# Experts' lists in a routed feed-forward kernel: rounding up to 128 rows in place of 256

## The chip, the cores and the metric

The kernel runs on one core of one Trainium2 chip. The metric is the device time of one execution in microseconds, the median of several. A profile of one execution goes with it: a span from the first to the last instruction, busy times by engine, and a trace of every instruction.

## What is computed

The reference is one block of a network on 4 sequences of 2048 tokens with 256 features. A time-mixing stage of two layers is followed by a layer norm; then comes a mixture of eight experts, and another layer norm. The expert part is what the change touches:

```python
gate_out = jnp.einsum('bsd,ed->bse', x, Wg)
top_v, top_i = jax.lax.top_k(gate_out, 2)
probs = jax.nn.softmax(top_v, axis=-1)
for e in range(8):
    w_e = jnp.sum(probs * (top_i == e), axis=-1)
    h1 = jnp.einsum('bsd,hd->bsh', x, W1[e])     # 256 -> 512
    h2 = jnp.einsum('bsd,hd->bsh', x, W2[e])     # 256 -> 512
    g = h1 * jax.nn.sigmoid(h1) * h2
    y = jnp.einsum('bsh,dh->bsd', g, W3[e])      # 512 -> 256
    out = out + y * w_e[..., None]
```

Each of the 8192 tokens goes to two experts, so there are 16384 (token, expert) pairs, and how many fall to one expert depends on the data.

## The kernel before, in words

Three phases follow each other: `attention_phase`, `expert_phase`, `norm_phase`. In the first one the router writes every pair (row number, share) into a list per expert in device memory (`slot_list`, 8192 places for each expert). `expert_phase` (line 969) works through these lists in blocks of rows that belong to one expert.

**Blocks.** There are 20 large blocks of 512 rows (`BIG`, line 51), and behind them 31 blocks of 256, 51 in all (`BLOCKS`, line 53). Each expert's list is rounded up to 256 rows. Those numbers are fixed when the program is built; which expert and which part of its list a block takes comes from a small table that VectorE computes (`big_table`, `small_counts`, `fill_table`, lines 117 to 168) and SP reads with `value_load`. Blocks that no expert needs read filler rows and run like the others.

**One block.** GpSimd gathers its rows by an indirect DMA per 128 rows (`gather_rows`, line 83), TensorE transposes them (line 1301), ScalarE rounds them to a high part (`x_hi`) and VectorE subtracts that to get the low part (`x_lo`). Weights are split in the same way, in three parts of 512 KB each (`w_half` on ScalarE, line 1145, and `w_low` on VectorE, line 1198). Each product is then three matmuls: high by high, high by low, low by high. In `hidden` (line 1263) the weights are stationary and the block's rows are the moving side: 48 matmuls of 512 columns for a large block, 48 of 256 columns for a block of 256. So the gated product comes out with the hidden feature on the partitions, which is how the output products (lines 1312 to 1326) want it as their stationary side: 12 matmuls of 256 columns for each 128 rows. A unit is 512 columns of hidden product; a large block has four, a block of 256 has two. The unit's two halves use two of the four banks of `ring`, `silu` and `gated` have two buffers each, and `gate`, `g_hi`, `g_lo` follow on VectorE, ScalarE and VectorE. `weigh` (line 1221) multiplies the output rows by the pairs' shares, and GpSimd adds them to `x_acc` by indirect DMAs, one for 128 rows (line 1126).

**Order of the work.** Every engine runs the same steps, `step(s, ...)`. In step s TensorE does the hidden products of block s, the transposes of block s+1, then the output products of block s-1:

```python
pe.wait_ge(s_xg[1 - j], moved(half + j, tiles))   # line 1295: rows of block s+1
```

GpSimd, in step s, issues the gather for block s+1, and then the adds of block s-2; these wait until the adds of block s-3 have landed (line 1122) and until block s-2 has been weighed (line 1123):

```python
gather_rows(nc, pool, kept, x_src, s_met, half + j, 1 - j, size(1))
if within(s, 2, BLOCKS + 1):
    if within(s, 3, BLOCKS + 1):
        pool.wait_ge(s_add[1 - j], moved(half - 2 + j, size(-3)))
    pool.wait_ge(s_yv, out_banks(s - 1, size(-1)))
```

SP, in step s, issues the list entries and the first two weight parts of block s+2, then the list entries for the adds of block s-1 (after the adds of block s-3 have landed), then the third weight part of block s+2. ScalarE and VectorE keep to a fixed order of their own within the step (lines 1165 and 1229).

The steps at the beginning, at the change of size and at the end are written out; two loops of two steps each cover the rest of the large blocks and the rest of the blocks of 256 (`run`, line 1011).

Of the kernel before, what the change touches and what calls it, by code (L numbers as in the profile page):

```python
# [25 lines left out]
P = 128  # L26
ALU = mybir.AluOpType
# [10 lines left out]
E, H = 8, 512  # L38
# [14 lines left out]
BLOCKS = BIG + (2 * TOKENS - E) // SMALL + E - BIG * (CH // SMALL)  # L53
# [55 lines left out]
def whole_blocks(nc, dve, k, add, bits):  # L109

    table_link(dve, k, nc.vector.tensor_tensor(k.used[:, :], k.base[0:1, :], k.start[:, :], ALU.subtract))
    table_link(dve, k, nc.vector.tensor_scalar(k.used_i[:, :], k.used[:, :], float(add), None, ALU.add))
    table_link(dve, k, nc.vector.tensor_scalar(k.used_i[:, :], k.used_i[:, :], bits, None, ALU.logical_shift_right))
    table_link(dve, k, nc.vector.tensor_copy(k.full[:, :], k.used_i[:, :]))


def fill_table(nc, dve, k, kind, first, n, slots):

    by_expert = [1, n, E]
    past, hop = k.past[:, first:first + n, :], k.hop[:, first:first + n, :]  # L120
    w_row, slot_row = k.rows[:, 0, first:first + n], k.rows[:, 1, first:first + n]
# [9 lines left out]
    table_link(dve, k, nc.vector.scalar_tensor_tensor(slot_row, k.block_no[:, 0:n], float(slots), slot_row,  # L131
                                                      ALU.mult, ALU.add))
    if kind:

        table_link(dve, k, nc.vector.scalar_tensor_tensor(slot_row, k.taken[:, 0:1].to_broadcast([1, n]), float(CH), slot_row,
                                                          ALU.mult, ALU.add))

        table_link(dve, k, nc.vector.tensor_scalar(slot_row, slot_row, float(E * LIST), None, ALU.min))
    nc.vector.tensor_copy(k.table[:, 1, first:first + n], slot_row).then_inc(k.s_table, 1)


def big_table(nc, dve, k):

    dve.wait_ge(k.s_tab, 3)
    whole_blocks(nc, dve, k, 0, CH.bit_length() - 1)
    running_sum(nc, dve, k, k.end[:, 0, :], k.full[:, :])
    table_link(dve, k, nc.vector.memset(k.taken[:, :], 0.0))

    table_link(dve, k, nc.vector.tensor_tensor(k.before[:, :], k.end[:, 0, :], k.full[:, :], ALU.subtract))
    table_link(dve, k, nc.vector.tensor_scalar(k.before[:, :], k.before[:, :], -1.0, float(BIG), ALU.mult, ALU.add))  # L150
    table_link(dve, k, nc.vector.tensor_scalar(k.before[:, :], k.before[:, :], 0.0, None, ALU.max))
    table_link(dve, k, nc.vector.tensor_tensor(k.taken[:, 0:E], k.before[:, :], k.full[:, :], ALU.min))
    running_sum(nc, dve, k, k.end[:, 0, :], k.taken[:, 0:E])
    table_link(dve, k, nc.vector.tensor_scalar(k.skip[:, 0, :], k.taken[:, 0:E], -float(CH), float(LIST), ALU.mult, ALU.add))
    fill_table(nc, dve, k, 0, 0, BIG, CH)


def small_counts(nc, dve, k):

    whole_blocks(nc, dve, k, SMALL - 1, SMALL.bit_length() - 1)  # L160
    table_link(dve, k, nc.vector.scalar_tensor_tensor(k.used[:, :], k.taken[:, 0:E], -float(CH // SMALL), k.full[:, :],
                                                      ALU.mult, ALU.add))
    running_sum(nc, dve, k, k.end[:, 1, :], k.used[:, :])

    table_link(dve, k, nc.vector.scalar_tensor_tensor(k.skip[:, 1, :], k.taken[:, 1:E + 1], float(CH), k.skip[:, 0, :],
                                                      ALU.mult, ALU.add))
    table_link(dve, k, nc.vector.scalar_tensor_tensor(k.skip[:, 1, :], k.used[:, :], -float(SMALL), k.skip[:, 1, :],
                                                      ALU.mult, ALU.add))
# [800 lines left out]
def expert_phase(nc, w_ffn, x_src, x_acc, slot_list, kept):  # L969
    ident, table, pair_in, xg = kept.ident, kept.table, kept.pair_in, kept.xg  # L970
    s_w, s_pair, s_xg = kept.s_w, kept.s_pair, kept.s_xg
    with ExitStack() as ctx:
# [30 lines left out]
        s_h, s_silu, s_g, s_gh, s_gl = sem("h_product"), sem("silu_ready"), sem("gated_ready"), sem("gh_ready"), sem("gl_ready")  # L1003
        s_y, s_yv = sem("y_product"), sem("y_weighted")
# [4 lines left out]
        block = ctx.enter_context(nc.Block())  # L1009

        def run(eng, step):
# [4 lines left out]
            def peeled(first, end):  # L1016
                for s in range(first, end):
                    step(s, s // 2, s % 2, lambda d: Q if s + d < BIG else Q // 2)

            def loop(first, end, size):  # L1020
                with eng.Fori(first // 2, end // 2) as it:
                    step(it * 2, it, 0, size)
                    step(it * 2 + 1, it, 1, size)

            last = (BLOCKS - 2) // 2 * 2
            peeled(-1, 4)
            loop(4, BIG - 2, lambda d: Q)
            peeled(BIG - 2, BIG + 4)
            loop(BIG + 4, last, lambda d: Q // 2)
            peeled(last, BLOCKS + 2)  # L1030

        def banks_before(b, tiles, full):

            if isinstance(b, int):
                return full * min(b, BIG) + full // 2 * max(b - BIG, 0)
            return b * full if tiles == Q else b * (full // 2) + full // 2 * BIG

        def hidden_units(b, tiles):

            return banks_before(b, tiles, HC)  # L1040

        def row_units(b, tiles):

            return banks_before(b, tiles, DC)

        def out_banks(b, tiles):

            return banks_before(b, tiles, 2)

# [458 lines left out]
```

## Time and profile before

| | |
|---|---|
| Median of three runs | 1239.77 us (1239.7 to 1246.08) |
| Profiled execution | 1232.79 us, span 1230.9 us |
| TensorE busy | 1112.7 us (90%), weight loads 987.3 us (80%) |
| VectorE, ScalarE, GpSimd busy | 916.7 us (74%), 622.2 us (51%), 696.8 us (57%) |
| Expert phase | from about 530 to 1180 us of the span |
| Indirect DMAs in it | 142 gathers, 142 adds |

A busy TensorE is not TensorE at its peak: its instructions overlap, so rates are read from the distance between the starts of two matmuls. The granted clock of TensorE is 1.00 at 2.4 GHz and 0.50 at 1.2 GHz. An instruction of GpSimd that starts an indirect DMA is shown as long as the issue takes; when the data has landed shows at whoever waits for it.

### The profile page before, as it was taken

What the parts mean: (1) busy time and instruction counts of PE and PEld (TensorE: products, weight loads), DVE (VectorE), ACT (ScalarE), POOL (GpSimd) and SP (SyncE); (2) the same over time, 40 slices, a digit from 0 to 9 for tenths busy, and PEclk for the clock granted to TensorE, in tenths of its full rate; (3) what the DMA queues carried; (4) which work ended last, traced back from release to release, by engine and by line L of the source; (5) the groups of instructions that cost most, each with busy time, mean ns of one, the idle gap of its engine ahead of it and who ended that gap; (6) DMA issues with size and microseconds to landing.
All of it is one profiled execution on the core that took longest, in us unless ns stands there. A gap on an engine that the chain in (4) does not pass through costs nothing. (4 is left out here: it accounts for less than half of the span.)

```text
span 1230.9 us, 22912 instructions
## 1 busy us (share of the span) xinstructions
PE 1112.7 (90%) x6916; PEld 987.3 (80%) x6916; DVE 916.7 (74%) x2031; ACT 622.2 (51%) x1027; POOL 696.8 (57%) x572
## 2 busy tenths in 40 slices
PE   6999999999999998669999999999999999999900
PEld 6778877777777786558888888888989999999900
DVE  5788888888888886656766666666668887888737
ACT  4344454444444443254544454445456665666528
POOL 1012544444444543676666766677577776777634
PEclk9999999999999999779999999999999999999965
DMA  4011222111121111467665765576579988889559
GB/s 154 18 52 52 52 52 53 52 55 53 60 54 52 51 35 36 121 148 192 144 153 138 166 156 136 142 169 157 126 186 232 242 223 226 244 227 244 117 175 388
DMA packets 80660, 164.17 MB, mean 133 GB/s; under 512 B 27424, under 2 KB 45600, under 8 KB 80352
## 3 DMA queue, kind: packets, MB, share of 16 engines
q1 hardware_dynamic: 49248, 126.16, 33.9%
q0 software_dynamic: 31360, 37.38, 16.2%
q8 instruction: 25, 0.41, 0.2%
q14 instruction: 27, 0.22, 0.1%
HBM read 118.01 MB, written 45.49 MB: 133 GB/s over the span
## 5 line engine op out<-in xcount | busy, mean ns | idle before, releaser
L1126 POOL DMA_INDIRECT x_acc<-fy_sb,pair_out x142 | 285.6, 2012 | 149.4 <-DVE fy_sb L1227 68.9
L1282 PE MATMUL fring<-fxh,fw_hi 128*128 128x256 f32 (+1 forms) x816 | 265.9, 326 | 3.6 <-DVE fxl L1218 2.0
L1284 PE MATMUL fring<-fxh,fw_lo 128*128 128x256 f32 (+1 forms) x816 | 266.2, 326 | 0.0
L1283 PE MATMUL fring<-fxl,fw_hi 128*128 128x256 f32 (+1 forms) x816 | 265.6, 325 | 0.0
L1145 ACT ACTIVATE fw_hi<-w_raw 128x1024 fp32r<-128x1024 f32 x153 | 161.2, 1054 | 148.4 <-PE fy L1325 140.1
L1198 DVE TENSOR_TENSOR fw_lo<-w_raw,fw_hi 128x1024 fp32r<-128x1024 f32 x153 | 186.5, 1219 | 17.4 <-ACT fw_hi L1145 17.3
L509 POOL TENSOR_TENSOR rs<-ve,neg_half 128x4 f32<-128x4 f32 x48 | 55.6, 1158 | 253.8 <-DVE nm L596 253.8
L88 POOL DMA_INDIRECT xg<-x_src,pair_in x142 | 159.9, 1126 | 43.3 <-issue 42.1
L78 POOL DMA_INDIRECT slot_list<-pairs,slot_u x128 | 145.5, 1137 | 50.9 <-issue 35.2
L1282 PEld LDWEIGHTS fring<-fxh,fw_hi 128*128 128x128 f32 x816 | 154.0, 189 | 17.0 <-ACT fxh L1163 4.2
L1283 PEld LDWEIGHTS fring<-fxl,fw_hi 128*128 128x128 f32 x816 | 154.2, 189 | 13.3
L1284 PEld LDWEIGHTS fring<-fxh,fw_lo 128*128 128x128 f32 x816 | 154.2, 189 | 13.2
L1323 PE MATMUL fy<-fw_hi,gh 128*128 128x256 f32 x568 | 164.0, 289 | 0.0
L833 PE MATMUL ring<-xh,w_hi 128*128 128x512 f32 x384 | 160.6, 418 | 2.2 <-issue 2.0
L1325 PE MATMUL fy<-fw_hi,gl 128*128 128x256 f32 x568 | 159.8, 281 | 0.0
L1324 PE MATMUL fy<-fw_lo,gh 128*128 128x256 f32 x568 | 159.8, 281 | 0.0
L834 PE MATMUL ring<-xl,w_hi 128*128 128x512 f32 x384 | 153.5, 400 | 0.0
L835 PE MATMUL ring<-xh,w_lo 128*128 128x512 f32 x384 | 153.2, 399 | 0.0
L1207 DVE TENSOR_TENSOR gated<-fring,silu 128x512 f32<-128x512 f32 x142 | 98.2, 691 | 70.0 <-PE fring L1284 70.0
L1158 ACT ACTIVATE gh<-gated 128x512 fp32r<-128x512 f32 x142 | 89.6, 631 | 82.8 <-DVE gated L1207 82.8
L1212 DVE TENSOR_TENSOR gl<-gated,gh 128x512 fp32r<-128x512 f32 x142 | 97.4, 686 | 15.4 <-ACT gh L1158 15.4
L1324 PEld LDWEIGHTS fy<-fw_lo,gh 128*128 128x128 f32 x568 | 108.7, 191 | 0.0
(135 smaller groups left out, 1966.2 us busy)
## 6 DMA issues: line engine op xcount, KB each, us to landing
w_raw<-w_ffn SPq DMA_DIRECT2D x153, 512.0 KB, 4.7
x_in<-h SPq DMA_DIRECT2D x16, 512.0 KB, 3.4
x_src<-x SPq DMA_DIRECT2D x16, 512.0 KB, 4.5
x_acc<-x SPq DMA_DIRECT2D x16, 512.0 KB, 5.7
acc<-x_acc SPq DMA_DIRECT2D x16, 512.0 KB, 7.5
out<-o SPq DMA_DIRECT2D x16, 512.0 KB, 6.5
xg<-x_src,pair_in POOLq DMA_INDIRECT x142
x_acc<-fy_sb,pair_out POOLq DMA_INDIRECT x142
```

What stands on the lines that cost most here:

```text
L88: nc.gpsimd.indirect_dma_start(kept.xg[j][:, q, :], None, x_src, bass.IndirectOffsetOnAxis(kept.pair_in[j][:, q, 0:1].bitcast(U32), 0)).th ...
L833: nc.tensor.matmul(out, hi, xh[l][:, dc, :], start=dc == 0, stop=False)
L834: nc.tensor.matmul(out, hi, xl[l][:, dc, :], start=False, stop=False)
L1126: nc.gpsimd.indirect_dma_start(x_acc, bass.IndirectOffsetOnAxis(pair_out[j][:, q, 0:1].bitcast(U32), 0), y[j][:, q, :], None, compute_op=A ...
L1145: nc.scalar.activation(w_hi[:, j, low:high], w_raw[:, j, low:high], ACT.Copy).then_inc(s_whi[i], 1)
L1198: nc.vector.tensor_tensor(w_lo[:, j, low:high], w_raw[:, j, low:high], w_hi[:, j, low:high].bitcast(F32), ALU.subtract).then_inc(s_wlo[i], 1)
L1282: nc.tensor.matmul(out, hi, rows_hi, start=dc == 0, stop=False)
L1283: nc.tensor.matmul(out, hi, rows_lo, start=False, stop=False)
L1284: last = nc.tensor.matmul(out, lo, rows_hi, start=False, stop=dc == DC - 1)
L1323: nc.tensor.matmul(out, a, hi, start=hc == 0, stop=False)
L1324: nc.tensor.matmul(out, a, lo, start=False, stop=False)
L1325: last = nc.tensor.matmul(out, c, hi, start=False, stop=hc == HC - 1)
```

## The change

The lists are rounded up to 128 rows. At most 135 blocks of 128 rows can then be needed; they are laid out as 20 blocks of 512, 24 of 256 and 8 of 128 (136 tiles of 128 rows in place of 142). The order is: six large blocks; eight times one large block and one single of 128; six large blocks; the 24 of 256. That makes 52 blocks, with singles at 7, 9, ... 21.

In a single the sides of the hidden product are swapped: its rows are stationary and the weights move, 512 columns at a time, so that a half takes 6 matmuls and fills one bank. The gated product then has rows on the partitions, and TensorE transposes it in four pieces into ring bank 2 at the end of the step, behind the output products of the block before; ScalarE and VectorE take the high and the low part from there. The output products of a single are 12 matmuls.

The counts that the waits need are now computed from the list of sizes (class `Spot`); the table has three kinds of blocks, filled in steps 3 and 4 by VectorE. The order of operations on GpSimd and SP within a step stays as it was. The diff, cut to its core:

```diff
+TILES_MAX = (2 * TOKENS + E * (P - 1)) // P
+SINGLES = E
+PAIRS = (TILES_MAX - BIG * Q - SINGLES + 1) // 2
+SIZES = [Q] * 6 + [Q, 1] * SINGLES + [Q] * (BIG - SINGLES - 6) + [2] * PAIRS
+BLOCKS = len(SIZES)
+UNITS = {Q: HC, 2: HC // 2, 1: 1}
+ROW_BANKS = {Q: DC, 2: 1, 1: 1}
+OUT_BANKS = {Q: 2, 2: 1, 1: 1}
...
         def _(pool):
...
                     if within(s, 1, BLOCKS):
-                        pool.wait_ge(s_pt, row_units(s, size(0)))
-                    gather_rows(nc, pool, kept, x_src, s_met, half + j, 1 - j, size(1))
+                        pool.wait_ge(s_pt, spot.before(ROW_BANKS, 0))
+                    gather_rows(nc, pool, kept, x_src, s_met, half + j, 1 - j, spot.size(1))
                 if within(s, 2, BLOCKS + 1):
...
-                        pool.wait_ge(s_add[1 - j], moved(half - 2 + j, size(-3)))
-                    pool.wait_ge(s_yv, out_banks(s - 1, size(-1)))
+                        pool.wait_ge(s_add[1 - j], spot.moved(-3))
+                    pool.wait_ge(s_yv, spot.before(OUT_BANKS, -1))
...
+            def g_hi(b, j, u, spot):
+                v = spot.before(UNITS, 0) + u
+                if spot.size(0) == 1:
+                    act.wait_ge(s_gt, spot.before({Q: 0, 2: 0, 1: 1}, 1))
+                    src = ring[2][:, :]
...
+            def g_lo(j, u, spot):
+                dve.wait_ge(s_gh, spot.before(UNITS, 0) + u + 1)
+                src = ring[2][:, :] if spot.size(0) == 1 else gated[:, u % 2, :]
...
                 if within(s, 1, BLOCKS):
-                    weigh(s - 1, half - 1 + j, 1 - j, size(-1))
+                    weigh(half - 1 + j, 1 - j, spot)
+                if units == 1:
+                    g_lo(j, 0, spot)
                 if at(s, 2):
-                    small_counts(nc, dve, kept)
+                    rest_counts(nc, dve, kept)
                 if at(s, 3):
-                    fill_table(nc, dve, kept, 1, BIG, BLOCKS - BIG, SMALL)
+                    rest_starts(nc, dve, kept)
+                    fill_table(nc, dve, kept, 1)
+                if at(s, 4):
+                    fill_table(nc, dve, kept, 2)
...
+                        behind = u == 0 and spot.size(-1) == 1
                         if i == 0:
-                            pe.wait_ge(s_silu, v - 1)
+                            pe.wait_ge(s_silu, v if behind else v - 1)
+                            if u == 1 and spot.size(-1) == 1:
+                                pe.wait_ge(s_gl, v - 1)
...
+                    if tiles == 1:
+                        out = ring[i][:, :]
+                        for dc in range(DC):
+                            col = PART[i][0] + dc * H
+                            hi, lo = w_hi[:, j, col:col + H], w_lo[:, j, col:col + H]
+                            rows_hi, rows_lo = xh[:, dc * P:(dc + 1) * P], xl[:, dc * P:(dc + 1) * P]
+                            nc.tensor.matmul(out, rows_hi, hi, start=dc == 0, stop=False)
+                            nc.tensor.matmul(out, rows_hi, lo, start=False, stop=False)
+                            last = nc.tensor.matmul(out, rows_lo, hi, start=False, stop=dc == DC - 1)
+                        last.then_inc(s_h, 1)
+                        continue
...
+                if within(s, 0, BLOCKS - 1) and spot.size(0) == 1:
+                    pe.wait_ge(s_g, spot.before(UNITS, 1))
+                    for hc in range(HC):
+                        last = nc.tensor.transpose(ring[2][:, hc * P:(hc + 1) * P], gated[:, 0, hc * P:(hc + 1) * P], ident[:, :])
+                    last.then_inc(s_gt, 1)
```

## Rows read from the trace of the kernel before

**Rows 1.** Busy time by stretch: PE, PEld, DVE, ACT, POOL, PEclk, DMA share, GB/s

```profile
545.00:895.00 350.00, 347.86 (x2091) 307.41 (x2090) 230.70 (x317) 171.49 (x259) 240.81 (x159) 1.00 0.64 151
930.00:1170.00 240.00, 238.25 (x2029) 237.59 (x2028) 194.80 (x239) 151.63 (x210) 172.38 (x104) 1.00 0.84 217
```

**Rows 2.** Who waited for whom, TensorE, 545 to 1180: total, times, longest

```profile
PE ftp L1301 <- DMA xg<-x_src,pair_in: 5.2, 4, 3.1
PE fring L1282 <- ACT fxh L1163: 1.6, 1, 1.6
```

**Rows 3.** Timeline of TensorE, one large step: start, duration, instruction

```profile
673.25 0.39 PE L1282 MATMUL fring<-fxh,fw_hi 128*128 128x512 f32 x1
...
684.24 1.03 PE L1301 MATMUL ftp<-ident,xg 128*128 128x128 f32 x8
685.03 0.36 PE L1323 MATMUL fy<-fw_hi,gh 128*128 128x256 f32 x1
...
690.76 0.40 PE L1282 MATMUL fring<-fxh,fw_hi 128*128 128x512 f32 x1
```

**Rows 4.** Timeline of VectorE: weighing instructions four blocks of 256 apart

```profile
926.94 0.69 DVE L1227 TENSOR_TENSOR fy_sb<-fy,pair_out 128x512 f32<-128x512 f32 x1
...
962.63 0.68 DVE L1227 TENSOR_TENSOR fy_sb<-fy,pair_out 128x512 f32<-128x512 f32 x1
```

**Rows 5.** Timeline of VectorE: first table instruction of step 3, next weight split

```profile
603.97 0.39 DVE L123 TENSOR_TENSOR past<-block_no,end 1x248 f32<-1x248 f32 x1
...
606.87 1.23 DVE L1198 TENSOR_TENSOR fw_lo<-w_raw,fw_hi 128x1024 fp32r<-128x1024 f32 x1
```

**Rows 6.** Timeline of VectorE and GpSimd behind that large step

```profile
690.96 0.69 DVE L1227 TENSOR_TENSOR fy_sb<-fy,pair_out 128x512 f32<-128x512 f32 x1 [2.13 <-PE fy L1325]
...
692.50 2.27 POOL L1126 DMA_INDIRECT x_acc<-fy_sb,pair_out  x1 [3.04 <-issue]
...
706.25 0.95 POOL L88 DMA_INDIRECT xg<-x_src,pair_in  x1 [0.30 <-issue]
```

**Rows 7.** Timeline of GpSimd and TensorE, from large blocks to blocks of 256

```profile
885.02 2.35 POOL L1126 DMA_INDIRECT x_acc<-fy_sb,pair_out  x1 [5.50 <-DVE fy_sb L1227]
...
898.73 2.65 POOL L1126 DMA_INDIRECT x_acc<-fy_sb,pair_out  x1 [2.66 <-DMA x_acc<-fy_sb,pair_out]
...
909.99 0.98 POOL L88 DMA_INDIRECT xg<-x_src,pair_in  x1 [0.30 <-issue]
...
909.49 0.28 PE L1284 MATMUL fring<-fxh,fw_lo 128*128 128x256 f32 x1
912.84 0.66 PE L1301 MATMUL ftp<-ident,xg 128*128 128x128 f32 x4 [3.07 <-DMA xg<-x_src,pair_in]
```

**Rows 8.** Timeline of GpSimd and TensorE, a later wait among blocks of 256

```profile
1017.85 1.76 POOL L88 DMA_INDIRECT xg<-x_src,pair_in  x1 [0.30 <-issue]
...
1022.98 0.66 PE L1301 MATMUL ftp<-ident,xg 128*128 128x128 f32 x4 [0.93 <-DMA xg<-x_src,pair_in]
```

**Rows 9.** Timeline of SP's DMA queue during the wait in rows 7

```profile
911.52 0.33 SPq L1078 DMA_DIRECT2D w_raw<-w_ffn  x1
```

**Rows 10.** Busy time by stretch (columns of rows 1) and TensorE's timeline, behind that wait

```profile
914.00:917.00 3.00, 3.00 (x16) 3.00 (x15) 2.42 (x3) 0.65 (x2) 2.56 (x2) 0.50 1.07 195
917.00:918.00 1.00, 1.00 (x8) 1.00 (x8) 0.05 (x1) 0.00 (x0) 0.83 (x1) 0.78 0.97 366
...
914.66 0.42 PE L1323 MATMUL fy<-fw_hi,gh 128*128 128x256 f32 x1
...
916.58 0.42 PE L1323 MATMUL fy<-fw_hi,gh 128*128 128x256 f32 x1
```

**Rows 11.** TensorE's timeline and busy time by stretch, the second large block

```profile
548.00 1.10 PE L1301 MATMUL ftp<-ident,xg 128*128 128x128 f32 x8 [0.52 <-DMA xg<-x_src,pair_in]
550.71 0.47 PE L1282 MATMUL fring<-fxh,fw_hi 128*128 128x512 f32 x1 [1.62 <-ACT fxh L1163]
...
547.00:551.00 4.00, 1.86 (x12) 1.20 (x11) 2.37 (x4) 2.31 (x4) 3.08 (x4) 1.00 0.23 10
```

More of the change, by code:

```diff
@@ L1025, in run @@
+            mixed_end = 6 + 2 * SINGLES
+            pairs_from = BLOCKS - PAIRS
             last = (BLOCKS - 2) // 2 * 2
[L1026 to L1029, printed above, removed]
+            peeled(-1, 10)
+            loop(10, mixed_end - 2)
+            peeled(mixed_end - 2, pairs_from + 4)
+            loop(pairs_from + 4, last)
             peeled(last, BLOCKS + 2)
[L1032 to L1036, printed above, removed]
@@ L1069, in pairs @@
+            def pairs(spot, d, dst, j, done):
+                tiles = spot.size(d)
+                row = first_row(1, spot, d, SLOTS - CH)
                 return sp.dma_start(dst[j][:, 0:tiles, :], slot_list[bass.ds(row, tiles * P), :]
@@ L1160, in x_hi @@
[L1160 to L1166 removed]
+            def g_hi(b, j, u, spot):
+                v = spot.before(UNITS, 0) + u
+                if spot.size(0) == 1:
+                    act.wait_ge(s_gt, spot.before({Q: 0, 2: 0, 1: 1}, 1))
+                    src = ring[2][:, :]
+                else:
+                    act.wait_ge(s_g, v + 1)
+                    src = gated[:, u % 2, :]
+                if within(b, 2, BLOCKS):
+                    act.wait_ge(s_y, spot.before(OUT_BANKS, -1))
+                nc.scalar.activation(gh[:, j, u * CH:(u + 1) * CH], src, ACT.Copy).then_inc(s_gh, 1)
@@ new lines, in x_hi, with step @@
+            def x_hi(spot, d):
+                for i in range(ROW_BANKS[spot.size(d)]):
+                    n = width(spot.size(d))
+                    act.wait_ge(s_pt, spot.before(ROW_BANKS, d) + i + 1)
+                    nc.scalar.activation(xh[:, i * n:(i + 1) * n], tp[i][:, 0:n], ACT.Copy).then_inc(s_xh, 1)
+            def step(s, half, j, spot):
+                here, nxt = within(s, 0, BLOCKS - 1), within(s, -1, BLOCKS - 2)
+                units = UNITS[spot.size(0)] if here else 0
@@ L1229, in step @@
-            def step(s, half, j, size):
-                here, nxt, units = within(s, 0, BLOCKS - 1), within(s, -1, BLOCKS - 2), unit_count(size(0))
+                for k in range(OUT_BANKS[tiles]):
+                    bank, n = (j if tiles == 2 else k), min(tiles, 2)
+                    dve.wait_ge(s_y, spot.before(OUT_BANKS, -1) + k + 1)
+                    share = pair_out[j][:, 2 * k:2 * k + n, 1:2].bitcast(F32).to_broadcast([P, n, D])
+                    nc.vector.tensor_tensor(y[j][:, 2 * k:2 * k + n, :], yp[bank][:, 0:n, :], share, ALU.mult).then_inc(s_yv, 1)
@@ L1231, in step @@
+            def step(s, half, j, spot):
+                here, nxt = within(s, 0, BLOCKS - 1), within(s, -1, BLOCKS - 2)
+                units = UNITS[spot.size(0)] if here else 0
                 if here:
                     w_low(2, s, j)
-                    gate(s, 0, size(0))
+                    gate(s, 0, spot)
                 if nxt:
                     w_low(0, s + 1, 1 - j)
-                if here:
-                    g_lo(s, j, 0, size(0))
-                    gate(s, 1, size(0))
@@ L1239, in step @@
[L1239 to L1251 removed]
+                if units > 1:
+                    g_lo(j, 0, spot)
+                    gate(s, 1, spot)
```

307 lines of the change are left out of this document (163 added, 144 removed).

## The prediction

> **What bounds the kernel now.** I read the table of busy time by stretch first. The change touches only the expert stage, and there TensorE is busy in 347.86 of 350 us while blocks of 512 rows run and in 238.25 of 240 us while blocks of 256 run, at the full clock in both [rows 1]; DMA queues and VectorE have room (shares of 0.64 and 0.84, 230.70 us and 194.80 us). So a block costs what its matmuls cost, unless TensorE has to wait. The waits list says on what: 5.2 us in all, in four waits, the longest 3.1 us, always for gathered rows (xg) [rows 2]. I read the change from those two ends: how many matmuls go, and which gathers come too late.
>
> One step of a large block is then read from TensorE's timeline [rows 3]: the hidden products start at 673.25 and end where the transposes start, 684.24 (10.99 us, 48 matmuls of 512 columns, 0.229 us each); the eight transposes take 0.79 us; the output products of the block before run from 685.03 to 690.76 (5.73 us, 48 matmuls of 256 columns, 0.119 us each). The step is 17.51 us. In the stretch of 256-row blocks the weighing instruction comes at 926.94 and, four blocks later, at 962.63 [rows 4]: 8.92 us for a block.
>
> **What is removed and added on TensorE.** 31 blocks of 256 become 24, so 7 x 8.92 = 62.4 us go. Eight blocks of 128 come. Each has 12 matmuls of 512 columns (12 x 0.229 = 2.75), 12 of 256 (12 x 0.119 = 1.43), two transposes of its rows (a quarter of 0.79, 0.20) and four of the gated product (half of 0.79, 0.40): 4.78 us, eight of them 38.2 us. On TensorE alone the change is worth 38.2 - 62.4 = -24.2 us.
>
> **What hides the rest of a small block.** A single block still loads, splits and subtracts whole expert weights. VectorE works 230.70/350 x 17.51 = 11.5 us in a large step and 194.80/240 x 8.92 = 7.2 us in one of 256; a single has no more than the latter, so a pair of steps (large, single) has at most 18.7 us of VectorE work in 22.3 us of TensorE work. For the DMA queues the same reckoning gives 11.2 + 7.5 = 18.7 us. Neither ends last. The gated product of a single goes to ring bank 2 only after the output products of the large block before it (5.73 us), long after its gate; its high and low parts (one ScalarE and one VectorE instruction) are due before the next block's second unit, 12 matmuls of 0.229 us later; I cost that wait at nothing, and at under 1 us if VectorE is late. The table for the rest of the lists was a run of small VectorE instructions from 603.97 to the next weight split at 606.87 [rows 5], with no TensorE wait in that stretch [rows 2]; the new third step has 20 such instructions in place of 10, most of them on 8 elements. I cost them at nothing too, and at 1 us if they push a gate past the unit that needs its bank.
>
> **What is late: the gather behind the adds.** GpSimd issues, in order, the gather for block s+1 and then the adds of block s-2 (lines 1113 to 1128). A gather therefore stands behind the adds of the step before. In a large step the second weighing starts at 690.96, the four adds follow at 692.50 and the four gathers behind them end at 706.25 + 0.95 = 707.20 [rows 6]: 1.54 + 14.70 us. There the rows are needed only after the next large hidden product, so nothing waits. At the one place where steps become short, the first blocks of 256, it does wait: GpSimd's last gather begins at 909.99 and is issued by 910.97, TensorE has been done since 909.77 (909.49 + 0.28) and starts its transposes at 912.84, 1.87 us after the issue's end [rows 7]. The new order makes such a place of each single. After a large block A and a single B, the large block C is wanted at the end of B's hidden product, and its gather stands behind the four adds of the large block before A.
>
> I work the loop from second weighing to second weighing. The gather path: 1.54 + 14.70 (adds and gathers) + 1.87 (landing) + 0.79 (transposes of C) + 5.73 (output products of A) + 0.20 (to its second weighing, 690.96 against 690.76) = 24.83 us. TensorE's own path for the same two steps is 17.51 + 4.78 = 22.29 us. So TensorE waits 2.5 us in each such pair of steps. The first single (block 7) is free: block 5 before its neighbour is large, so the step of block 6 lasts 10.99 + 0.20 + 5.73 = 16.9 us, and the gather for block 8 has landed 18.1 us after the weighing at that step's start, 1.3 us before TensorE asks for it. The second (block 9) pays more: the adds of block 6 must wait until those of block 5 have landed, and between two such starts 13.71 us passed (885.02 to 898.73) [rows 7]. From the second weighing of block 5: 1.54 + 13.71 + 14.70 + 1.87 = 31.8 us until block 10 has its rows; TensorE is ready after -0.20 + 2.75 + 0.79 + 5.73 + 0.40 (single 7's step) + 10.99 + 0.20 + 1.43 + 2.75 (large 8, single 9) = 24.8 us: a wait of 7.0 us. Sum of waits: 7.0 + 6 x 2.5 = 22.0 us. The landing is the term with bounds. While weights crowd the queues in the 256-row stretch, a gather begun at 1017.85 and issued by 1019.61 let TensorE go at 1022.98, 3.37 us [rows 8]; I take 1.87, since in the new steps as in [rows 7] just one weight part is issued beside the gather (at 911.52 there) [rows 9]. The bounds are 7 x 1.5 = +10.5 us above and, for adds and gathers that are issued 1 us sooner, 7 us below.
>
> The Trainium skill (DMA: Bandwidth & Descriptors, Anatomy of one DMA) puts a GpSimd-issued DMA at about 2.0 us plus its bytes over 436 GB/s, an estimate of 2.3 us for one gather of 128 KB. [Rows 7] show 2.85 us from the beginning of the last gather to the transposes, so the trace is slower than the page; by the page every wait would be 0.55 us shorter and the sum below 3.9 us lower, and the measurement decides.
>
> **What a wait does to the clock.** After the wait of 3.07 us the granted clock fell to 0.50 from 914 to 917 and was 0.78 in the next microsecond, so 3.4 us at 1.2 in place of 2.4 GHz [rows 10]; matmuls of 256 columns then started 0.213 us apart (914.66 to 916.58, nine of them), so 16 of them cost 16 x (0.213 - 0.119) = 1.5 us more. Two idle times of 0.52 and 1.62 us close to each other left the clock at 1.00 from 547 to 551 [rows 11]. The 7.0 us wait will pay 1.5 us. The six of 2.5 us lie about midway between 2.14 and 3.07 us, so I let half of them pay: 4 x 1.5 = 6.0 us in all, with 1.5 and 10.5 us as ends.
>
> **Sum.** -62.4 + 38.2 + 22.0 + 6.0 = +3.8 us. The profiled execution took 1232.79 us around a span of 1230.9; the median of the runs is 1239.77, 7 us above it. I lay the difference on the median: 1243.6 us. A difference of 0.5% (6.2 us) is about what a measurement of this kernel can tell from no change.
>
> **Rivals.** (1) The clock falls at every wait and the gathers land as late as in the 256-row stretch. All seven pay: 7 x 1.5 = 10.5 in place of 6.0 gives +8.3, 1248 us; with landings later by 1.5 us it is up to +18.8, 1258.6 us. For it: 2.5 us is not far from 3.07. Against it: 2.5 us is shorter than the one wait that a fall followed, and the queues are less full here. It decides from the point where five or more of the six waits pay. The Trainium skill (TensorE: Matmul & The Clock Gate, HAM oscillation) describes a kernel whose clock falls at each wait for a transfer, tile after tile; by that rule all seven pay. Chance 0.37.
> (2) The waits don't form, or only the first does, because the adds are issued faster once the steps alternate, or a gather lands while the last transposes of the single run. Without any wait the time is 1239.8 - 24.2 = 1215.6 us; with waits of half the size and the first one's clock, -24.2 + 11.0 + 1.5 = -11.7, 1228 us. For it: TensorE's work does go. Against it: the wait at 909.77 happened in this very order of instructions, with only two gathers behind the four adds. Chance 0.20.
> (3) The forecast, within about 6 us of before: 0.43. That the change does less than it says is no case: the number of blocks of each size is fixed when the program is built, and empty ones run like full ones.
>
> The forecast's own range is 1236 to 1246 us. Eight times in ten the time should lie between 1226 us (half the waits) and 1257 us (all clocks, most landings late). Faster by over 0.5%: 0.20; within: 0.43; slower: 0.37.
>
> **What would show it.** In the changed profile TensorE should be at full clock and busy through the six leading large blocks and the first single, then idle about 7 us for xg in the step of block 9 and about 2.5 us in each of six more single steps, with clock of 0.5 after some; waits of TensorE for xg should sum to some 25 us instead of 5.2. Between the starts of two runs of four adds some 24.8 to 26.5 us should pass. The stretch of 24 blocks should keep 8.9 us a block. I am wrong if TensorE waits for something else (split weights, the low part of the gated product), if the gathers are in time, or if a single block's own matmuls take more than 4.8 us.

## The result, and the profile after

The changed kernel takes 1229.22 us (median of 20 runs, 1220.58 to 1235.75) beside 1241.59 us of the kernel before on the same chip (20 runs): a ratio of 0.9897, 95% interval 0.9879 to 0.9915. That is 12.4 us less, where 3.8 us more was forecast; 1229.22 us lies outside the forecast's own range (1236 to 1246 us), though inside the wide one (1226 to 1257 us). The profiled execution took 1233.89 us, span 1232.0 us; it holds one stop of 13 us, which the last of the experiments takes up, and without it would have been faster than the median.

Busy time by stretch, the columns as in [rows 1]:

```profile
545.00:895.00 350.00, 327.71 (x1902) 285.02 (x1901) 237.56 (x347) 177.44 (x263) 208.86 (x151) 0.97 0.66 169
930.00:1170.00 240.00, 236.19 (x1964) 232.78 (x1963) 185.83 (x228) 145.25 (x201) 167.22 (x102) 0.99 0.80 203
```

TensorE is no longer busy all through the 350 us of the first stretch; 22 us of it are idle. The waits list of the expert stage says where (in all, times, longest):

```profile
PE fring L1366 <- ACT fxh L1223: 13.1, 1, 13.1
PE ftp L1385 <- DMA xg<-x_src,pair_in: 12.1, 9, 6.8
```

13.1 us are the one stop. Gathered rows cost 12.1 us in nine waits, one of them 6.8 us, against the 25 us that the prediction wanted to see. TensorE's timeline has the long wait just where it was forecast, in the step of the second single, and shows what became of the others:

```profile
702.19 1.97 PE L1385 MATMUL ftp<-ident,xg 128*128 128x128 f32 x8 [6.82 <-DMA xg<-x_src,pair_in]
...
734.33 0.60 PE L1417 MATMUL fring<-ident,gated 128*128 128x128 f32 x4
...
750.90 1.09 PE L1385 MATMUL ftp<-ident,xg 128*128 128x128 f32 x8 [0.28 <-DMA xg<-x_src,pair_in]
751.75 0.36 PE L1409 MATMUL fy<-fw_hi,gh 128*128 128x256 f32 x1
...
757.49 0.60 PE L1417 MATMUL fring<-ident,gated 128*128 128x128 f32 x4
```

The first wait is 6.82 us (forecast 7.0), and the eight transposes behind it take 1.97 us at the lower clock instead of 1.09. But the ones after it are 0.27, 0.28, 0.29, 0.20, 0.34 and 0.32 us (forecast 2.5 each). From one transposition of the gated product to the next, 734.33 to 757.49, a pair of steps takes 23.16 us. GpSimd's timeline of that pair, with VectorE's under it, shows why:

```profile
736.26 1.58 POOL L1176 DMA_INDIRECT x_acc<-fy_sb,pair_out  x1 [6.72 <-issue]
738.15 1.56 POOL L1176 DMA_INDIRECT x_acc<-fy_sb,pair_out  x1 [0.30 <-issue]
740.02 1.72 POOL L1176 DMA_INDIRECT x_acc<-fy_sb,pair_out  x1 [0.30 <-issue]
742.04 1.84 POOL L1176 DMA_INDIRECT x_acc<-fy_sb,pair_out  x1 [0.30 <-issue]
744.19 1.01 POOL L98 DMA_INDIRECT xg<-x_src,pair_in  x1 [0.30 <-issue]
...
748.03 0.99 POOL L98 DMA_INDIRECT xg<-x_src,pair_in  x1 [0.30 <-issue]
```

```profile
734.53 0.69 DVE L1291 TENSOR_TENSOR fy_sb<-fy,pair_out 128x512 f32<-128x512 f32 x1 [1.23 <-PE fy L1411]
735.60 0.69 DVE L1273 TENSOR_TENSOR gl<-fring,gh 128x512 fp32r<-128x512 f32 x1 [0.38 <-ACT gh L1217]
736.55 1.23 DVE L1258 TENSOR_TENSOR fw_lo<-w_raw,fw_hi 128x1024 fp32r<-128x1024 f32 x1 [0.26 <-ACT fw_hi L1196]
```

Four adds and four gathers take 12.76 us here (736.26 to 748.03 + 0.99), and 12.76 to 12.97 us in all six of the steps with a short wait, not the 14.70 us of [rows 6]. The add that took 2.27 us there takes 1.58 us here.

### The profile page after: what moved, and what is told of

It reads as the page before. It is cut to its first block and busy times, and to the rows that moved or that the text cites. A ratio compares the mean times of both kernels' runs of the same rounds, so it can differ in the third digit from the quotient of the medians.

```text
span 1232.0 us, 21935 instructions
## 1 busy us (share of the span) xinstructions
PE 1094.7 (89%) x6624; PEld 959.7 (78%) x6624; DVE 913.2 (74%) x2050; ACT 618.3 (50%) x1019; POOL 657.9 (53%) x560
## 5 line engine op out<-in xcount | busy, mean ns | idle before, releaser
L1176 POOL DMA_INDIRECT x_acc<-fy_sb,pair_out x136 | 258.8, 1903 | 187.0 <-DVE fy_sb L1291 103.0
L1366 PE MATMUL fring<-fxh,fw_hi 128*128 128x256 f32 (+1 forms) x704 | 234.9, 334 | 15.3 <-ACT fxh L1223 13.1
L1368 PE MATMUL fring<-fxh,fw_lo 128*128 128x256 f32 (+1 forms) x704 | 233.9, 332 | 0.0
L1367 PE MATMUL fring<-fxl,fw_hi 128*128 128x256 f32 (+1 forms) x704 | 233.3, 331 | 0.0
L98 POOL DMA_INDIRECT xg<-x_src,pair_in x136 | 148.7, 1093 | 44.4 <-issue 39.6
L1366 PEld LDWEIGHTS fring<-fxh,fw_hi 128*128 128x128 f32 x704 | 133.2, 189 | 29.0 <-ACT fxh L1223 13.3
L1368 PEld LDWEIGHTS fring<-fxh,fw_lo 128*128 128x128 f32 x704 | 133.1, 189 | 13.5
L1367 PEld LDWEIGHTS fring<-fxl,fw_hi 128*128 128x128 f32 x704 | 133.0, 189 | 13.1
L1217 ACT ACTIVATE gh<-gated 128x512 fp32r<-128x512 f32 x128 | 80.8, 631 | 81.2 <-DVE gated L1267 76.9
L1409 PEld LDWEIGHTS fy<-fw_hi,gh 128*128 128x128 f32 x544 | 104.1, 191 | 0.0
```

The source lines that it names most:

```text
L1176: nc.gpsimd.indirect_dma_start(x_acc, bass.IndirectOffsetOnAxis(pair_out[j][:, q, 0:1].bitcast(U32), 0), y[j][:, q, :], None, compute_op=A ...
L1366: nc.tensor.matmul(out, hi, rows_hi, start=dc == 0, stop=False)
L1367: nc.tensor.matmul(out, hi, rows_lo, start=False, stop=False)
L1368: last = nc.tensor.matmul(out, lo, rows_hi, start=False, stop=dc == DC - 1)
L1409: nc.tensor.matmul(out, a, hi, start=hc == 0, stop=False)
```

## The experiments

**Does the issue of an add depend on VectorE, or on the queues?** These are VectorE's splits of the weights (fw_lo) and GpSimd's adds behind [rows 6], in the kernel before:

```profile
692.06 1.23 DVE L1198 TENSOR_TENSOR fw_lo<-w_raw,fw_hi 128x1024 fp32r<-128x1024 f32 x1 [0.40 <-ACT fw_hi L1145]
694.55 1.22 DVE L1198 TENSOR_TENSOR fw_lo<-w_raw,fw_hi 128x1024 fp32r<-128x1024 f32 x1
697.33 1.22 DVE L1198 TENSOR_TENSOR fw_lo<-w_raw,fw_hi 128x1024 fp32r<-128x1024 f32 x1
```

```profile
695.08 2.15 POOL L1126 DMA_INDIRECT x_acc<-fy_sb,pair_out  x1 [0.30 <-issue]
697.53 2.45 POOL L1126 DMA_INDIRECT x_acc<-fy_sb,pair_out  x1 [0.30 <-issue]
700.29 1.55 POOL L1126 DMA_INDIRECT x_acc<-fy_sb,pair_out  x1 [0.30 <-issue]
```

The add at 692.50 starts while the split (692.06 + 1.23) has 0.79 us to go and takes 2.27 us; with 0.69 us left an add takes 2.15, with 1.02 left 2.45, and with no such instruction running 1.55. In the changed kernel the low part of the single's product (gl at 735.60) comes ahead of the split on VectorE, and its high part (gh) comes ahead of the rounding of the weights on ScalarE (fw_hi), for which the split then waits 0.26 us. So the split starts 0.29 us after the add. Theory T1 makes what is left of VectorE's instruction the cause; T2 blames the weights on the DMA queues. T1's edit leaves most of the split out:

```diff
 def w_low(i, b, j):
     low, high = PART[i]
+    if not (isinstance(b, int) and b < 2):
+        high = low + 64
     dve.wait_ge(s_whi[i], b + 1)
     ...
```

> The kernel before, with VectorE's subtraction for the low parts of the weights cut to 64 columns from the third block on (most of the low weights are left out, so the products lack their low terms). Theory T1 (an add's issue on GpSimd takes about 1.55 us plus what is left of a VectorE instruction with two SBUF operands that is running when it starts): adds of 1.55 to 1.6 us all through the large blocks instead of 2.27, 2.15, 2.45, 1.55, and from the start of the first add to the end of the last gather about 12.5 us instead of 14.7. Theory T2 (crowded DMA queues lengthen the issue): unchanged, 14.5 to 14.7 us. The time itself should move little by either, by at most some 3 us, since TensorE's instructions stay.

T2's edit leaves most of the weights' transfers out:

```diff
 def weights(b, j, i, w_row):
     low, high = PART[i]
     if within(b, 2, BLOCKS):
...
+        high = low + 64
```

> The kernel before, with each weight transfer cut to 64 columns per part from the third block on (most of the weights are not loaded, so the products are of other weights). T2 (crowded DMA queues lengthen the adds' issue): adds and gathers of a large step about 12.5 us instead of 14.7. T1 (VectorE's two-operand instructions do): 14.5 to 14.7 us as before. The landing of the gathers in the 256-row stretch, up to 3.37 us from issue's end to TensorE's start, should fall towards 1.9 us by either, if crowding is its cause.

GpSimd's timeline of a large step, with the short split (the first fence, with one row of VectorE's under it) and with the short transfers (the last):

```profile
700.05 1.62 POOL L1126 DMA_INDIRECT x_acc<-fy_sb,pair_out  x1 [4.29 <-issue]
701.97 1.59 POOL L1126 DMA_INDIRECT x_acc<-fy_sb,pair_out  x1 [0.30 <-issue]
...
705.73 2.05 POOL L1126 DMA_INDIRECT x_acc<-fy_sb,pair_out  x1 [0.30 <-issue]
...
711.94 0.94 POOL L88 DMA_INDIRECT xg<-x_src,pair_in  x1 [0.30 <-issue]
```

```profile
705.66 0.69 DVE L1214 TENSOR_TENSOR gl<-gated,gh 128x512 fp32r<-128x512 f32 x1 [0.57 <-ACT gh L1158]
```

```profile
694.34 2.27 POOL L1127 DMA_INDIRECT x_acc<-fy_sb,pair_out  x1 [3.04 <-issue]
696.92 2.15 POOL L1127 DMA_INDIRECT x_acc<-fy_sb,pair_out  x1 [0.30 <-issue]
699.37 2.45 POOL L1127 DMA_INDIRECT x_acc<-fy_sb,pair_out  x1 [0.30 <-issue]
702.13 1.55 POOL L1127 DMA_INDIRECT x_acc<-fy_sb,pair_out  x1 [0.30 <-issue]
...
708.09 0.95 POOL L88 DMA_INDIRECT xg<-x_src,pair_in  x1 [0.31 <-issue]
```

With hardly any weights in the queues (busy for 0.40 of 720 to 860 us, not 0.64) the four adds keep their durations to the hundredth of a microsecond, and the whole is 14.70 us again: T2 falls. The landing may depend on the queues: after one wait of 1.89 us at the first blocks of 256 none follows, where three profiles of the kernel before with whole transfers have two or three more, of 0.55 to 1.92 us. With one profile this is likely, and not shown. With the short split the first three adds are 1.56 to 1.62 us and the whole 12.83 us (13.22 and 13.03 in the steps beside it): T1 stands. The fourth add, 2.05 us, started while another VectorE instruction with both operands in SBUF (gl from gated and gh) had 0.62 us left. So the rule is 1.55 us plus what is left of it, less about 0.1 us; I had expected 12.5 us because I had counted the split alone. Over all fourteen profiles the rule has its counterpart too: 218 adds of the expert phase start beside a VectorE instruction with an operand in PSUM, and they take 1.55 to 1.63 us. The times, 1236.42 and 1231.65 us beside 1234.46, say nothing more, as expected.

The Trainium skill (SBUF — State Buffer, SBUF: two separate sides) says that VectorE and GpSimd share a port pair as an exclusive lock, and that a VectorE instruction with two SBUF inputs takes it only against a GpSimd instruction that reads SBUF. That a DMA issued by GpSimd can't get its descriptors written is told there of VectorE's 2-port modes, and not of such an instruction. These rows agree with a lock held to the instruction's end (2.05 us beside 0.62 us left), and show it for the issue of an indirect DMA, which the Trainium skill doesn't name there; no run here tells what in the issue needs the lock.

**The same in the changed kernel.** The edit is that of the short split. GpSimd's timeline has two rows of VectorE's under it.

> The changed kernel with VectorE's subtraction for the low weights cut to 64 columns from the third block on (most of the low weights are left out). Theory T1 (the add's issue is lengthened by VectorE's two-operand instructions): from the first add to the end of the last gather in an alternating pair of steps about 12.3 us instead of 12.76, so the six waits of 0.3 us vanish; the first wait falls from 6.8 to about 3 to 5 us, since the large steps before it lose some 2 us of adds each. If waits and issue times stay as they are, T1 has no part in them in this order of steps.

```profile
733.55 1.58 POOL L1176 DMA_INDIRECT x_acc<-fy_sb,pair_out  x1 [7.03 <-issue]
735.43 1.56 POOL L1176 DMA_INDIRECT x_acc<-fy_sb,pair_out  x1 [0.30 <-issue]
737.30 1.55 POOL L1176 DMA_INDIRECT x_acc<-fy_sb,pair_out  x1 [0.30 <-issue]
739.15 1.55 POOL L1176 DMA_INDIRECT x_acc<-fy_sb,pair_out  x1 [0.30 <-issue]
741.01 1.02 POOL L98 DMA_INDIRECT xg<-x_src,pair_in  x1 [0.30 <-issue]
742.33 1.27 POOL L98 DMA_INDIRECT xg<-x_src,pair_in  x1 [0.30 <-issue]
...
745.16 1.15 POOL L98 DMA_INDIRECT xg<-x_src,pair_in  x1 [0.30 <-issue]
```

```profile
735.17 0.69 DVE L1269 TENSOR_TENSOR gated<-fring,silu 128x512 f32<-128x512 f32 x1 [1.11 <-PE fring L1370]
...
742.05 0.69 DVE L1275 TENSOR_TENSOR gl<-gated,gh 128x512 fp32r<-128x512 f32 x1 [0.70 <-issue]
```

All four adds are at the floor, 6.24 us instead of 6.70, as T1 has it; the second starts 0.26 us into a gated (735.17 + 0.69), which reads one operand from PSUM, and isn't lengthened. But the sum is 12.76 us again, the waits stay at 0.25 to 0.40 us and the first falls to 5.83 us only: the gathers now start 0.47 us sooner, and the second met a gl with 0.41 us left (1.27 us instead of 0.98). My numbers for the waits were wrong, since I moved the adds and left the gathers where they were. So in this order of steps a shorter split gains nothing: what the adds save, the gathers lose again. (The one execution took 1226.28 us, with a stop of 11.74 us of the kind told below.)

**Do the late gathers make the waits?** Here the gather for the block behind each single, and behind the first block of 256, goes out one step earlier, ahead of that step's adds:

```diff
-if within(s, 0, BLOCKS - 2):
+if within(s, 0, BLOCKS - 2) and not (spot.size(0) == 1 or spot.block == BLOCKS - PAIRS):
     ...
     gather_rows(nc, pool, kept, x_src, s_met, half + j, 1 - j, spot.size(1))
+if spot.size(1) == 1 or spot.block == BLOCKS - PAIRS - 1:
+    pool.wait_ge(s_pt, spot.before(ROW_BANKS, 1))
+    gather_rows(nc, pool, kept, x_src, s_met, half + 1, j, spot.size(2))
```

> The changed kernel with the gather for the block behind each single, and behind the first block of 256, issued one step earlier on GpSimd, ahead of that step's adds. Theory G (the gathers behind the adds are what TensorE still waits for): the waits of 6.8, six of 0.3 and 3.0 us vanish and with them the two falls of the clock, 2 x 1.5 us by the price of the prediction: about 14 us less than the changed kernel, some 1215 us, at least 10 us less if the clock gives back less. Rival (the adds, issued up to 6 us later, hold up the ring of outputs or the lists): a new wait on VectorE's outputs or on the next adds, and a time within 5 us of the changed kernel's, 1225 to 1232 us.

> The kernel with the early gathers at all singles once more, beside the changed kernel on the same chip. Theory G: it beats the changed kernel by the first wait and its clock, 6.6 + 2.2 us, less some 0.5 us for the new waits on the low part of the gated product (2.2 us against 1.6 us of the six small waits): about 8 us less. Rival (the ratio 0.9813 beside 0.9897 came from another chip and call): within 3 us of the changed kernel.

> The changed kernel unaltered, beside the three others and on their chip. Some 12 us less than the kernel before (ratio 0.988 to 0.992). By the account from the traces: 63.6 us less in the stretch of 256, 40.5 us for eight singles, 8.2 us of waits and 2.2 us of clock: 12.7 us less.

The first run gave 1213.15 us, a ratio of 0.9813 (0.9767 to 0.9859). The second gave 1217.25 us, 0.9808 (0.9756 to 0.986), and the changed kernel beside it 1224.18 us, 0.986 (0.9812 to 0.9909). That is 6.9 us less than the changed kernel on the same chip (six runs each, 1214.64 to 1225.04 and 1220.0 to 1228.06 us), the fastest version of all, and half of the 14 us that I had expected of the first run. (The changed kernel's own third run, 0.986, is lower than the 0.988 to 0.992 that I had expected, but these lie within its interval.) The wait of 6.8 us and the six small ones are gone and the clock is 1.00 through 680 to 860 us. From the transposes of block 2 to those of the first block of 256 that is 358.5 us (567.41 to 925.89) instead of 366.6 (565.92 to 932.53): 8.1 us, as theory G had it. Late gathers in the stretch of 256 take part of it back: 217.6 us in this profile and 215.9 in the first run's, 213.5 to 215.4 in the three of the changed kernel. The rival's wait forms too, but small. VectorE and TensorE of the second run:

```profile
739.25 1.29 DVE L1294 TENSOR_TENSOR fy_sb<-fy,pair_out 128x512 f32<-128x512 f32 x2 [3.88 <-DMA pair_out<-slot_list]
```

```profile
741.28 0.47 PE L1369 MATMUL fring<-fxh,fw_hi 128*128 128x512 f32 x1 [0.72 <-DVE gl L1276]
...
961.56 1.12 PE L1388 MATMUL ftp<-ident,xg 128*128 128x128 f32 x4 [3.08 <-DMA xg<-x_src,pair_in]
```

Since the adds go out later, the list for the next adds is loaded later (SP waits for them), the weighing waits 3.88 us for it, gl comes late, and TensorE pays 0.72 us. And the wait at the first blocks of 256 is still there, before the transposes of the fourth of them, where the changed kernel has it: the edit moved the gather of the second one.

**The early gather only where a long wait is left.** The conditions become the second single alone (s = 8) and the second to fourth block of 256.

> The changed kernel with the early gather, ahead of the adds, only where a long wait is left: for the block behind the second single, and for the second, third and fourth block of 256. Theory G (only the order of gathers and adds makes the waits of 6.4 to 6.8 and 3.0 us): both vanish, the six of 0.3 us stay, the clock stays at full speed through 680 to 720 us and at the first blocks of 256: some 13 us less than the changed kernel, 1204 to 1216 us beside a kernel before of 1234. Rival (the backlog of adds moves on): the waits come back one single or one block later, at half their size or more, as the wait of 3.08 us did in the run with the early gathers at all singles, and the time is that run's, 1213 us, or more.

```profile
715.18 1.97 PE L1389 MATMUL ftp<-ident,xg 128*128 128x128 f32 x8 [6.14 <-DMA xg<-x_src,pair_in]
...
977.84 0.66 PE L1389 MATMUL ftp<-ident,xg 128*128 128x128 f32 x4 [2.86 <-DMA xg<-x_src,pair_in]
```

1223.82 us, 0.9848 (0.9806 to 0.989): the rival was right. The wait only moves to the third single (6.14 us) and down the blocks of 256 (2.86 us, then 1.92). What is late is a backlog of adds: where the steps become short, a run of adds must wait until the one before has landed, as here in the changed kernel, and a gather that overtakes it leaves it for the next.

```profile
685.13 1.57 POOL L1176 DMA_INDIRECT x_acc<-fy_sb,pair_out  x1 [3.82 <-DMA x_acc<-fy_sb,pair_out]
```

**The forecast's waits, made by hand.** No wait of 2.5 us had formed, so the clock's price at such waits was still open. Memsets of a scratch tile on GpSimd ahead of the gather in each single step make them; the diff is that with two memsets of 128 x 1320, and a second run has one of 128 x 1700:

```diff
+if spot.size(0) == 1:
+    if within(s, 8, BLOCKS):
+        pool.wait_ge(s_idle, spot.before({Q: 0, 2: 0, 1: 2}, 0))
+    pool.sem_inc(s_met, 1)
+    for i in range(2):
+        nc.gpsimd.memset(idle[:, i, :], 0.0).then_inc(s_idle, 1)
 gather_rows(nc, pool, kept, x_src, s_met, half + j, 1 - j, spot.size(1))
```

> The changed kernel with two memsets of a scratch tile on GpSimd (128 x 1320 each, together about 2.5 us by the 0.96 us of a memset of 1032 elements in the trace) ahead of the gather in each of the eight single steps: it brings back by hand the 2 us that the prediction's adds and gathers had too many. If the gather path of the prediction is right, the six small waits become 0.3 + 2.4 = 2.7 us each and the first about 9 us, in all 7 x 2.4 = 17 us more than the changed kernel. Clock theory H1 (a wait of 2.5 to 2.9 us is paid by the clock in about half the cases, 1.5 us each): 17 + 4.5, about 21 us more. H2 (every wait pays): 17 + 9 = 26 us more. H3 (none but the first pays): 17 us more. Rival to the gather path (GpSimd has slack that takes the memsets up): waits stay near 0.3 us and the time stays.

> The changed kernel with one memset on GpSimd (128 x 1700) ahead of the gather in each single step, about 1.9 us by the 1.47 us that each 128 x 1320 took in the run with two. There two memsets of 2.94 us made each of six waits 3.7 us longer (4.0 to 4.6 us), and the clock fell after all six (granted 0.83 in the 20 us that hold a wait), 2.0 us for each. Here the six waits should be 2.2 to 2.9 us, the size that the prediction forecast. H1 (half of such waits are paid by the clock): three of the six large steps behind a wait are 1.4 to 2.6 us longer than 18.03 us. H2 (all are paid): all six. H3 (none below 2.86 us, the shortest with a fall so far; 1.92 us is the longest without one): none. By H2 the time is about 13 + 10 us above the changed kernel's, by H3 about 13.

GpSimd, TensorE and the clock with two memsets, the last with the columns of [rows 1]:

```profile
773.80 2.94 POOL L1173 MEMSET fidle<- 128x1320 f32 x2
```

```profile
785.16 1.97 PE L1392 MATMUL ftp<-ident,xg 128*128 128x128 f32 x8 [4.05 <-DMA xg<-x_src,pair_in]
```

```profile
785.00:787.00 2.00, 1.84 (x9) 1.85 (x10) 0.06 (x1) 0.60 (x1) 0.90 (x1) 0.50 0.82 111
```

TensorE with one memset:

```profile
746.07 1.09 PE L1392 MATMUL ftp<-ident,xg 128*128 128x128 f32 x8 [2.02 <-DMA xg<-x_src,pair_in]
774.01 1.26 PE L1392 MATMUL ftp<-ident,xg 128*128 128x128 f32 x8 [3.63 <-DMA xg<-x_src,pair_in]
```

With two memsets the ratio is 1.0152 (1.0096 to 1.0209), with one 1.0093 (1.0059 to 1.0126): both slower than before. GpSimd had no slack; the gather path was the limit, as the prediction had it. The first wait is 7.12 us with two memsets, where I had expected about 9, and 7.16 us with one. The six waits are 3.96 to 4.56 us with two memsets, and 2.45, 2.02, 3.63, 3.67, 3.79 and 3.73 us with one. Every large step behind one of these twelve waits is longer than the 18.03 us of the changed kernel, by 1.42 to 2.66 us with two memsets (mean 2.06) and 1.40 to 2.65 us with one (mean 1.67), those behind 2.45 and 2.02 us as well, and behind each of the twelve the granted clock falls to 0.50. So H2 (every such wait is paid by the clock) holds for this order of steps, though just two of the twelve waits are of the size that the prediction forecast.

The Trainium skill (TensorE: Matmul & The Clock Gate, HAM oscillation) describes this pattern, a clock that falls at each wait for a transfer, tile after tile; these twelve waits agree with it, and some waits among the blocks of 256, told at the end, don't.

The waits were longer than I expected, for two reasons: the two memsets took 2.94 us, not 2.5 (the single one 2.1, not 1.9), and the landing stretched. From the end of the last gather's issue to the transposes it is 1.88 us in the changed kernel (749.02 to 750.90), 2.68 us here (782.48 to 785.16), and with one memset 1.91 us at 746.07 and 3.52 us at 774.01 (770.49 before). I didn't find what makes the difference between those two.

**The stop at the start of the expert phase.** In the profiled execution of the changed kernel TensorE stood still at 551 to 564 us. A repeat of each kernel, unaltered, and the kernel before with its first eleven steps written out, ask whether the change makes it:

> The changed kernel once more, unaltered. Its first profiled execution held one stop of 13.1 us of all engines at 551 to 564 us, where the expert phase begins; the kernel before shows 1.62 us at that place. S1 (the stop's length varies from execution to execution, in both kernels): another length here, and the execution's time moves with it; without the stop, about 1221 us. S2 (the longer program of the changed kernel makes it): some 13 us again at the same place. Elsewhere the waits stay: 6.8 us in the step of the second single, six of about 0.3 us, 3.0 us at the first blocks of 256.

> The kernel before once more, unaltered, for a second profile. S1 (the stop where the expert phase begins varies in length in this program too): another length than 1.62 us at 548 to 575 us, up to 13 us, and the time with it. If instead it is always under 2 us here, the longer program of the changed kernel has a part in it. The late gathers of the 256-row stretch (0.7 to 1.1 us each at 1013 to 1042 us) may come at other places; if they are due to where the weights' transfers fall, they recur at the same blocks.

```diff
-peeled(-1, 4)
-loop(4, BIG - 2, lambda d: Q)
+peeled(-1, 10)
+loop(10, BIG - 2, lambda d: Q)
```

> The kernel before with its first eleven steps of the expert phase written out, as in the changed kernel, instead of five; the computation is the same, block for block. S2 (longer straight-line code makes the stop at the start of the expert phase longer): waits there of 4 to 13 us in the profile, as in the six profiles of kernels with eleven steps written out (2.5 to 13 us), and a time 3 to 5 us above the kernel before. S1 (it varies alike in both): a time within 2 us of the kernel before and a stop as in the profiles with five (1.6 to 5.7 us).

TensorE in the first profile of the changed kernel (the first line), and in the second:

```profile
564.25 0.76 PE L1366 MATMUL fring<-fxh,fw_hi 128*128 128x512 f32 x1 [13.12 <-ACT fxh L1223]
```

```profile
550.61 0.47 PE L1366 MATMUL fring<-fxh,fw_hi 128*128 128x512 f32 x1 [1.62 <-issue]
```

The second execution took 1217.43 us, with 1.62 and 0.87 us there, and its other waits as before (6.43 us, six of 0.17 to 0.32, 3.07). The kernel before took 1237.19 us (1.62 and 0.83 us); its late gathers of 256 rows came at 917 to 938 us this time (1.69, 1.12 and 0.55 us), so they keep to no block. With eleven steps written out it gave a ratio of 0.9978 (0.9937 to 1.002), so the longer straight code costs nothing that shows, and S1 is the better account. The stop varies between executions: single waits of 4 us and more at this place stand in four of the ten profiles with eleven steps written out (11.74 us in the changed kernel with the short split) and in one of the four with five (4.07 us in the kernel before with the short split).

## Why the prediction was wrong, point by point

Three profiles of each kernel (the changed one's first, second and third; those of the kernel before, of its repeat and of the one with eleven steps written out) give every term, measured from the transposes of block 2 to those of the first block of 256, and from there to the last:

| term | forecast | measured |
|---|---|---|
| seven blocks of 256 fewer | -62.4 | 279.0 to 214.6: -64.3 |
| eight singles | +38.2 | +40.4 |
| wait at the second single | +7.0 | +6.7 |
| six waits of singles | +15.0 | +1.6 |
| clock | +6.0 | +2.3 |
| sum | +3.8 | -13.3 |

The singles are what is left of 366.6 - 315.6 = 51.0 us after the three terms under them, 5.05 us each. The measured sum is next to the 12.4 us between the medians.

**The blocks of 256** were right. Of the 1.9 us more, 0.8 are waits for late gathers, as in [rows 8] (4.5 us in the kernel before, 3.7 in the changed one, means of three profiles). The rest is in TensorE's own steps: several blocks of the changed kernel take 8.62 to 8.85 us, not 8.92, and no run says why.

**The single's own matmuls** were forecast at 4.78 us and take 5.05, over the 4.8 us that the prediction named as a sign of being wrong. Two gaps are seen: 0.18 us pass before a single's first hidden matmul (747.59; the last output one starts at 747.29, and they start 0.12 us apart), and TensorE drains for 0.16 us more than I counted before the transposes. The other covers held: no wait for the split weights, the table or the low part of the gated product is in the list of waits.

**The first wait** was right, 6.82, 6.43 and 6.78 us, and so was the reckoning through the adds that wait for each other's landing. That the number is so close is in part luck: between the two starts 13.30 us pass (671.83 to 685.13; 13.71 forecast), adds and gathers take 14.17 (14.70), and the landing takes 2.89 (1.87), so that two terms too long and one too short cancel.

**The step that failed** is "14.70 (adds and gathers)" in the gather path of a pair of steps, taken from large steps [rows 6]. In the alternating order it is 12.76 us in the pair shown. The rest of that path held: 1.73 us from the weighing (734.53) to the adds (1.54 forecast), 1.88 for the landing (1.87), 0.85 for the transposes (0.79), 5.74 for the output products (5.73), 0.20 to the weighing: 23.16 us instead of 24.83. TensorE's own path is 23.16 - 0.28 = 22.88 us instead of 22.29. So the difference of 2.54 us shrinks by 1.67 and by 0.59 to 0.28 us, the wait that is seen. (Of the 0.59 us, 0.34 are the two gaps above; the rest lies in pieces of at most 0.12 us.) The 14.70 us was a duration with a condition: three of its four adds had started under VectorE's split of the weights. The change itself moves the split behind the first add, by the single's gh and gl in front of it. The kernel before showed the condition by itself: where the small instructions of the table hold its split up, until 0.61 us behind the first add, adds and gathers of a large step take 13.45 us (587.35 to 599.44 + 1.36), and 14.70 us is the longest of its large steps.

```profile
587.35 1.62 POOL L1126 DMA_INDIRECT x_acc<-fy_sb,pair_out  x1 [3.03 <-issue]
```

```profile
587.96 1.23 DVE L1198 TENSOR_TENSOR fw_lo<-w_raw,fw_hi 128x1024 fp32r<-128x1024 f32 x1
```

Rival (2) said this in words ("because the adds are issued faster once the steps alternate"), with a chance of 0.20 and no row for it, though VectorE's timeline at 692 us was at hand. That its -11.7 us is 0.7 us from the result is luck: it was worked out for waits of half the size, and what came is the whole first wait and almost nothing of the others.

**The clock** was wrong twice over, both times too cheap. The fall behind the first wait costs 2.41, 1.98 and 2.49 us in the three profiles (the large step is 20.44, 20.01 and 20.52 us instead of 18.03), not 1.5: after 702 us the granted clock is 0.50 to 706 and 0.57 to 708, longer than the 3.4 us of [rows 10], from which the price was taken. And waits of 2.5 us would probably all have paid, not half of them, as the runs with memsets show: with the waits as forecast the sum would have been nearer rival (1). Since they didn't form, only one was paid for, and the term came out below the forecast all the same. The clock of the changed kernel is 0.81 in the 20 us that begin at 700, and 1.00 from 720 to 860.

## What to carry to other kernels

The duration of an instruction on GpSimd that issues a DMA isn't a constant: read beside each one what VectorE is doing at its start, and ask whether the change moves that. Where two paths differ by some 10% (24.83 and 22.29 us here), a term taken from another stage decides the sign, so its spread (13.45 to 14.70 us here, in the kernel before alone) belongs in the sum and not at the edge of the range. A queue entry that overtakes a backlog moves the wait on; it goes away only where the backlog has room to drain, as in the steps that alternate.

## What the runs showed that was not expected

An add's issue on GpSimd is 1.55 us, plus what is left of a VectorE instruction with two operands in SBUF when it starts (2.27, 2.15 and 2.45 us for 0.79, 0.69 and 1.02 us), whatever the queues carry. Waits of TensorE of 2.02 to 4.56 us cost 1.4 to 2.7 us of clock where large steps and singles alternate, twelve times of twelve. Among blocks of 256 it is less plain: 1.79 us cost nothing (9.97 us to the next transposes, 1.13 of it the next wait, against 8.92), and in the run with few early gathers the step behind 2.86 us is no longer (10.75 less the next wait, 1.92) at a granted clock of 1.00, while the one behind that 1.92 us is 10.51, 1.6 us longer, at 0.50 for part of it; the expectation of the run with one memset had these two the wrong way round. And at the start of the expert phase TensorE can stand still for 1.6 to 13 us, differently in each execution of one kernel; VectorE, ScalarE and GpSimd are then waiting for something that the profile gives no name. What it is stays open.
